# Another order of the instructions of one attention unit, and one score matmul for two key/value groups in the first two query tiles

## What is computed

```
q = (x @ Wq).reshape(b, t, 32, 16).transpose(0, 2, 1, 3)
k = (x @ Wk).reshape(b, t, 8, 16).transpose(0, 2, 1, 3)
v = (x @ Wv).reshape(b, t, 8, 16).transpose(0, 2, 1, 3)
q, k = rope(q), rope(k)
scores = einsum('bhqd,bhkd->bhqk', q, repeat(k, 4)) / sqrt(16)
scores = where(causal, finfo.min, scores)
ctx = einsum('bhqk,bhkd->bhqd', softmax(scores), repeat(v, 4))
x = x + ctx.transpose(0, 2, 1, 3).reshape(b, t, 512) @ Wo
```

## Time and profile before

| | |
|---|---|
| median of 3 runs | 1407.05 us (1406.98 to 1407.35) |
| profiled execution, its own time | 1404.97 us |
| its span | 1403.1 us |
| PE busy, share of span | 1345.0 us, 96% |
| DVE, ACT, POOL busy | 1006.7, 718.6, 699.8 us |
| first matmul of `attend0` | at 58.1 us |
| last matmul of `attend0` | at 344.1 us |

### The profile page before, as it was taken

The page is one execution under the profiler, slowest core; times in us unless marked ns, Lnnn a source line. Parts: engine busy times, 40 slices in busy tenths (PEclk is TensorE's granted clock), DMA queues, the critical chain, the costliest instruction groups (busy, mean ns, idle before and its releaser), DMA issues. The chain is left out here.

```text
span 1403.1 us, 20386 instructions
## 1 busy us (share of the span) xinstructions
PE 1345.0 (96%) x6795; PEld 1076.5 (77%) x6795; DVE 1006.7 (72%) x2372; ACT 718.6 (51%) x1560; POOL 699.8 (50%) x619
## 2 busy tenths in 40 slices
PE   8999999987998999999999999999999999799999
PEld 5766666655676788888888888888888888688887
DVE  8888877775767878877787778777877788622322
ACT  3488886684544554544454545444545455433332
POOL 5589996683544554433542544335425442054453
PEclk9999999999999999999999999999999999999999
DMA  4000000100201011110110101101101010143332
GB/s 142 1 1 1 2 1 1 31 16 26 65 0 68 24 31 30 31 38 9 37 39 15 37 24 31 38 9 38 39 16 38 16 46 0 31 105 100 91 92 83
DMA packets 64950, 50.72 MB, mean 36 GB/s; under 512 B 5776, under 2 KB 54288, under 8 KB 64592
## 3 DMA queue, kind: packets, MB, share of 16 engines
q1 hardware_dynamic: 64848, 49.43, 12.2%
HBM read 47.32 MB, written 2.10 MB: 35 GB/s over the span
## 5 line engine op out<-in xcount | busy, mean ns | idle before, releaser
L1935 POOL TENSOR_TENSOR a_p_lo<-a_prob,a_p_hi 128x512 fp32r<-128x512 f32 x160 | 203.2, 1290 | 45.5 <-ACT a_p_hi L1789 44.0
L243 DVE CUSTOM_DVE_ANT_0 a_score<-a_score,mask_w 128x384 f32<-128x384 f32 (+3 forms) x384 | 195.9, 558 | 13.1 <-PE a_score L1386 11.4
L737 ACT ACTIVATE a_pt_hi<-a_ring 128x512 fp32r<-128x512 f32 x160 | 93.9, 596 | 164.3 <-PE a_ring L421 164.3
L890 POOL TENSOR_TENSOR a_rot_a<-a_rot_a,a_rot_b 128x512 f32<-128x512 f32 x79 | 102.3, 1296 | 147.5 <-DVE a_rot_b L599 147.5
L728 ACT ACTIVATE a_prob<-a_score,a_nmax 128x128 f32<-128x128 f32 (+3 forms) x256 | 132.0, 529 | 57.9 <-DVE a_nmax L243 57.8
L364 PE MATMUL a_xo<-h_hi,w_both 128*128 128x512 f32 x384 | 151.4, 394 | 2.7 <-PEq L1973 2.5
L366 PE MATMUL a_xo<-h_hi,w_both 128*128 128x512 f32 x384 | 150.9, 393 | 0.0
L365 PE MATMUL a_xo<-h_lo,w_both 128*128 128x512 f32 x384 | 150.2, 391 | 0.0
L2562 POOL TENSOR_TENSOR w_both<-raw,w_both 128x512 fp32r<-128x512 f32 (+2 forms) x63 | 87.1, 1407 | 116.0 <-ACT w_both L2506 115.9
L895 POOL TENSOR_TENSOR a_p_lo<-a_rot_a,a_p_hi 128x512 fp32r<-128x512 f32 x79 | 102.2, 1295 | 65.7 <-ACT a_p_hi L754 65.7
L579 DVE TENSOR_TENSOR a_pt_lo<-a_ring,a_pt_hi 128x512 fp32r<-128x512 f32 x160 | 108.5, 686 | 32.1 <-ACT a_pt_hi L737 31.2
(11 more groups left out here) (380 smaller groups left out, 3660.4 us busy)
## 6 DMA issues: line engine op xcount, KB each, us to landing
raw<-in_L_gate_up_t SPq DMA_DIRECT2D x40, 256.0 KB, 3.1
raw<-in_L_attn_wq SPq DMA_DIRECT2D x32, 256.0 KB, 2.8
raw<-in_L_attn_wo SPq DMA_DIRECT2D x32, 256.0 KB, 2.6
raw<-in_L_down_t SPq DMA_DIRECT2D x20, 256.0 KB, 2.6
raw<-in_L_attn_wk SPq DMA_DIRECT2D x8, 256.0 KB, 2.9
raw<-in_L_attn_wv SPq DMA_DIRECT2D x8, 256.0 KB, 2.9
out<-x SPq DMA_DIRECT2D x8, 256.0 KB, 2.2
x<-in_L_attn_x SPq DMA_DIRECT2D x3, 512.0 KB, 7.5
```

What stands on the lines that cost most here:

```text
L243: return nc.vector.tensor_tensor_reduce(scores, scores, m.mask_w[:, T - n:T], -1.0, LARGE, ALU.add, ALU.min, to)
L890: nc.gpsimd.tensor_tensor(of_a, of_a, of_b, ALU.add).then_inc(summed, 1)
L1935: nc.gpsimd.tensor_tensor(p_lo[:, mm % NP, :], prob[:, mm % NE, :], p_hi[:, mm % NP, :].bitcast(F32), ALU.subtract).then_inc(p_ready, 1)
```

## The change

Two score matmuls that share their stationary queries and differ only in the key/value group become one, whose moving operand holds both groups: in tile 0 a bank is now two matmuls of 256 columns where it was four of 128, in tile 1 one of 512 where it was two of 256. A bank now holds half as many heads, each for both groups, and DVE writes its maxima to other places of `nmax`. The number of banks and mask matmuls and all the columns stay. Then the four written-out orders change. What is shown of the orders is a part; in all four the calls are the same as before.

```diff
@@ tensor: scores @@
-                for h in range(per):
-                    nc.tensor.matmul(out[:, h * n:(h + 1) * n], q_rows[:, bank * per + h, :], k_rows[:, u % 2, x, 0:n],
-                                     start=(h == 0), stop=False)
+                heads = per // X2
+                first = (x * S_BANKS[i] + bank) * heads
+                for h in range(heads):
+                    to = out[:, X2 * h * n:X2 * (h + 1) * n].rearrange("p (x n) -> p x n", x=X2)
+                    nc.tensor.matmul(to, q_rows[:, first + h, :], k_rows[:, u % 2, 0:X2, 0:n], start=(h == 0), stop=False)
...
@@ tensor: order @@
                 if u:
                     turn_keys(u)
+                turn_back(u - 1, 1)
                 weigh(u - 1, 2, 0, 0)
-                turn_back(u - 1, 1)
...
@@ vector: maxima @@
-                nc.vector.tensor_reduce(nmax[:, i % 2, bank * per:(bank + 1) * per, x],
+                at = (x * S_BANKS[i] + bank) * per
+                nc.vector.tensor_reduce(nmax[:, i % 2, :, :].rearrange("p h x -> p (h x)")[:, at:at + per],
@@ vector: order @@
                 maxima(u, 2, 0, 0)
-                maxima(u, 2, 0, 1)
                 if first is not None:
                     low(first)
-                maxima(u, 2, 0, 2)
-                maxima(u, 2, 0, 3)
                 if tail:
                     low(QT)
                 take_heads(u - 1, 2)
+                maxima(u, 2, 0, 1)
+                maxima(u, 2, 0, 2)
+                maxima(u, 2, 0, 3)
...
-                if u == NU - 1:
-                    low_row(1)
-                    make_row(2)
                 take_heads(u, 0)
                 read_queries(u, 3)
                 read_heads(u, 1)
                 read_keys(u + 1)
                 take_heads(u, 1)
+                if u == NU - 1:
+                    low_row(1)
+                    make_row(2)
...
@@ scalar: order @@
-                exponentials(u, 3, 0, 2)
                 read_queries(u + 1, 2)
                 high(u, 3, 1, 1)
                 if ahead is not None:
                     tile_high(ahead)
-                high(u, 3, 0, 2)
+                exponentials(u, 3, 0, 2)
+                exponentials(u, 3, 1, 2)
...
@@ gpsimd @@
-                if k == 1:
+                if k == 0:
                     put_maxima(u, 2)
-                if k == 7:
+                if k == 6:
                     put_maxima(u, 3)
                 if k == 12:
                     put_maxima(u + 1, 0)
-                if k == 16:
+                if k == 15:
                     put_maxima(u + 1, 1)
```

More of the change, by code:

```diff
@@ L1532, in _ @@
                     turn_tile(first + 1)
-                weigh(u - 1, 3, 0, 2)
+                if tail:
+                    turn_tile(QT + 2)
                 turned_scores(u, 0, 1, 0)
@@ L1536, in _ @@
                 scores(u, 3, 0, 1)
+                turned_scores(u, 1, 0, 0)
                 scores(u, 3, 0, 2)
                 weigh(u - 1, 3, 1, 2)
-                if tail:
-                    turn_tile(QT + 2)
+                scores(u, 3, 0, 3)
                 weigh(u - 1, 3, 0, 3)
-                turned_scores(u, 1, 0, 0)
-                scores(u, 3, 0, 3)
+                turned_scores(u, 1, 1, 0)
+                weigh(u - 1, 3, 1, 3)
                 if u == NU - 1:
                     turn_rows(0)
-                turned_scores(u, 1, 1, 0)
-                weigh(u - 1, 3, 1, 3)
                 turn_queries(u, 2, 1)
+                scores(u, 3, 1, 0)
                 turned_scores(u, 1, 0, 1)
-                scores(u, 3, 1, 0)
+                turned_scores(u, 1, 1, 1)
+                turn_back(u - 1, 3)
                 weigh(u, 0, 0, 0)
-                turn_back(u - 1, 3)
                 if tail:
@@ L1561, in _ @@
                 scores(u, 3, 1, 3)
+                turn_queries(u + 1, 0, 0)
                 if first is not None:
@@ L1717, in _ @@
                     add_tile(first)
+                maxima(u, 3, 0, 0)
+                if first is not None:
+                    low(first + 1)
                 if u == NU - 1:
@@ L1720, in _ @@
                     make_row(0)
-                maxima(u, 3, 0, 0)
                 maxima(u, 3, 0, 1)
-                if first is not None:
-                    low(first + 1)
                 maxima(u, 3, 0, 2)
@@ L1728, in _ @@
                 read_queries(u, 2)
+                if u == 0:
+                    late_low()
                 if u == NU - 1:
@@ L1740, in _ @@
                     add_tile(QT + 3)
+                maxima(u, 3, 1, 1)
                 read_heads(u, 0)
-                maxima(u, 3, 1, 1)
                 maxima(u, 3, 1, 2)
```

89 lines of the change are left out of this document (43 added, 46 removed).

## The result

The changed kernel takes 1385.38 us (median of 4 runs, 1384.06 to 1385.76); the kernel before took 1407.01 us beside it. The ratio is 0.9848, with a 95% interval of 0.9836 to 0.9860. That is faster by 21.6 us, where 10.6 were forecast and the range ended at 1391. The profiled execution's span is 1382.3 us, against 1403.1. The attention function accounts for it: its last matmul ended 344.5 us after the first instruction before, and 323.8 us after it now, 20.7 us earlier.

The account below looks back on a forecast made before the run. The prediction took PE as the bound, with POOL almost as full in middle units. Its terms, 3.4 + 4.9 + 1.6 + 0.6 + 2.5 - 2.4 = 10.6 us, took 1407.05 to 1396.5 us; range 1391 to 1404.

Parts of the forecast that it names:

- The score matmuls: Tiles 0 and 1: merging saves PE 0.42 us per unit, all of it in tile 0; 3.4 us over 8 units.
- The rival by which the merge saves nothing: Score banks: by the isolated matmul gap the merge gains nothing, the order does its part; 1399.9 us, chance 0.04.
- The order at the boundaries: Unit ends and starts: earlier maxima from POOL and reordered starts remove waits, 0.7 us at 7 boundaries, 4.9 us.
- New waits: Tile 2: DVE's `take_heads` ahead of three maxima delays PE's scores, a loss of 0.3 us per unit, 2.4 us.
- rival 4: Tile 2: `take_heads` before the maxima makes PE's scores late and POOL run dry; slower, 1411 us, chance 0.07.
- Units 5 and 6: Units with the first projections: `turn_tile`'s wait for ACT gets covered, 0.8 us per unit, 1.6 us.
- The one stall that I booked: Units 5 and 6: `turn_tile` waits 0.78 us for ACT to empty `qkbank`; removal booked at 0.8 us per unit.
- Unit 7: `turn_rows(1)` waits less for a score bank, as DVE's `read_heads` now follows the maxima: 0.6 us.
- The tail: Output projection: earlier DVE chain before the second projection, 1.5 us, and shorter last waits, 1.0 us; together 2.5 us.
- rival 5: Tail: shorter waits keep PE's clock at 2.4 GHz, making the forecast 1394.8 us; chance 0.10.
- the second part: Tail's last weighings: an earlier weighing removes the 0.29 us waits and most of the 0.78 us; 1.0 us.
- Rival 1: All units: PE and POOL reach their floor, 27.2 us per unit; 17.5 us gained, 1389.6 us; chance 0.14 with a milder form.

Follow-up runs that it names:

- e1: Kernel before with only the merged score matmuls and the new places of their maxima, every engine's order as before: 1404.18 us, ratio 0.9985.
- e2: Changed kernel with the score matmuls of before, one for each head and group, new order kept: 1388.16 us, ratio 0.9864.
- e15: Changed kernel with GpSimd's numbers of before, so it writes the maxima one block later in three places: 1392.08 us, ratio 0.9898.
- e4: Merged matmuls everywhere, new order in loop bodies up to unit 4, order of before in units 5 to 7 and the tail: 1400.09 us, ratio 0.9952.
- e5: Changed kernel with VectorE's first-tile low part and taking of heads back behind tile 2's maxima: 1388.93 us, ratio 0.9868.
- e17: e1 with only VectorE's taking of a finished tile's heads moved ahead of three maxima of tile 2: 1416.80 us, ratio 1.0065.
- e9: e1 with one TensorE move in units 5 and 6, turning the output tile behind tile 3's first weighings and second-group scores: 1403.39 us, ratio 0.9972.
- e10: e9 with three more moves in units 5 and 6: tile 0's weighing later, VectorE's two low parts one maximum earlier: 1403.26 us, ratio 0.9976.
- e8: Changed kernel with ScalarE's list of before in all bodies: 1400.51 us, ratio 0.9958.
- e13: Changed kernel with one ScalarE step as before, a tile 3 exponential ahead of the next unit's third query tile copy: 1395.22 us, ratio 0.9917.
- e7: Changed kernel with VectorE's list of before in all bodies: 1391.63 us, ratio 0.9890.
- e11: Changed kernel with the order of before in the last loop body alone (end of unit 7, rest of the output projection): 1390.97 us, ratio 0.9885.
- e3: Merged matmuls everywhere, new order on all four engines in units 5 and 6 alone, order of before elsewhere: 1398.40 us, ratio 0.9943.

## Why the prediction was wrong

The direction and the middle unit were right; the sum was 11 us short, and the time fell below the range. The steps that failed: beside the projections it priced one wait of 0.8 us, where PE had 3.9 to 4.4 us to give in each body, and it gave ScalarE's list no term. By the bodies of the two traces, against the terms that fall to each: up to unit 4, 5.9 us where 3.4 were booked; units 5 and 6, 8.3 where 3.2; unit 7, 3.0 where 1.4; the tail, 3.5 where 2.5. Half of the miss is in units 5 and 6. By its own steps:

- **The score matmuls** (3.4 us booked): right in size on PE, 0.37 to 0.41 us a unit, and 2.2 (e1) to 2.8 us (e2) in the time. The rival by which the merge saves nothing falls. The isolated gap in the Trainium skill (TensorE: Matmul & The Clock Gate, Back-to-back issue gap) would have left the bank unchanged, since it goes by columns alone. The same section says that this gap is too short for few columns when each matmul brings its own weights, and gives about 81 ns per matmul of 128 columns for that case; the rows agree with the direction, and show about 110 ns here.
- **The order at the boundaries** (0.7 us each, 4.9): its reason was right and is now shown. GpSimd's later writing alone costs 6.7 us (e15), 5.7 by the traces, with the wait back in each unit, 0.8 us in the middle ones. Up to unit 4 the order gave 4.1 us (e4).
- **New waits** (2.4 us of loss booked): the wrong sign. VectorE's early heads are worth 3.5 us (e5, 3.1 by the traces). I priced VectorE's delay against PE's old neighbours; there it does cost, 12.6 us (e17), and rival 4's mechanism is real in that kernel. The new list of PE had made room.
- **Units 5 and 6** (1.6 us for both, 3.2 with their share of the other terms): measured 3.9 and 4.4, 8.3 us. The one stall that I booked was right to 0.15 us (e9). Four others, 1.5 us together, stood in the same timeline, and I didn't book them. Nor could they be taken one by one (e10): all lists together give 3.6 and 4.1 us over e1 in these bodies, but 0.7 and 0.6 with PE's list old, 1.0 and 1.3 with ScalarE's old, 2.7 and 3.2 with VectorE's old, 3.2 in both with GpSimd's old. PE and ScalarE have to move together.
- **ScalarE's list** had no term at all. It is worth 15.1 us beside the other new lists (e8), 9.8 of them one exponential that let the query copy pass (e13). This is the largest thing that the prediction lacked.
- **Unit 7** (0.6, and 0.8 by the common terms): 3.0 us by the trace. The 0.6 was right, 1.75 to 1.16 us. I booked nothing for the moments' place, and the wait behind them went from 2.10 to 0.48 us. VectorE's old list, which brings it back, costs 2.9 us in this body (e7), up to 1.7 of it the clock.
- **The tail** (2.5 us): 3.5 by the trace, and 4.6 when undone alone (e11), both with up to 1.7 of the clock, which stayed up as in rival 5. So the order itself gave 1.8 to 2.9 us. The low part before the second projection does come earlier, the wait is 0.98 for 2.26 us. Of the second part, 1.0 us, the wait of 0.29 went and the 0.78 stayed.

Rival 1 (both engines at their floor, 1389.6) was nearest, and had 0.14. Its mechanism was right for the middle units, and the projections' units went to the same floor: PE is busy in 33.82 of 33.90 us. My price for each wait came from one row, while the test that the profile offered was the sum: PE's need of 27.4 us, two projections of 2.8 and two transposes of 0.44 are 33.9 us, so a body of 38.3 had 4.4 us to give.

## What to carry to other kernels

When the order of a stage changes on every engine, size the gain by the stage: its length less the bounding engine's own work from start to start, not by the waits that one can name. Check each moved step against the new neighbours on the other engines, since the same step was worth 3.5 us in one set of lists and cost 12.6 in the other; and look in every list for an instruction that may wait with something urgent queued behind it. Where totals spread by a few us, compare bodies between anchors in the trace.

## What the runs showed of the hardware

- The granted clock fell in different places in runs of kernels with the same lists up to there (e1 and e3). A fall made body 1 of e3 1.6 us longer, and body 7 of e1, where PE has waits of its own, 0.5 us (34.26 for 33.79 in e9). The kernel before had one in the tail, behind a wait of 2.26 us; with 3.38 us of wait it fell too (e11), and with 0.98 there and 1.76 before the last projection it did not (after). e13's trace shows none in the attention at all, with 1.03 us of wait in each unit. What decides it stays open.
- After the change PE's waits in units 1 to 6 are 0.24 us at most, and POOL is busy for 26.6 of 27.2 us beside it in a middle unit. Two engines can both be at their floor at once, given lists that fit.
